# Seven of 36 probability tiles per group turned through memory instead of on TensorE

## The chip, the cores and the metric

One core of one Trainium2 chip runs the whole program. The metric is the device time of one launch in microseconds. The core has five engines that this text names by their short forms: PE (TensorE, matrix products), DVE (VectorE), ACT (ScalarE), POOL (GpSimd) and SP (SyncE, which issues DMAs). ACT can issue DMAs too, on a queue of its own.

## The reference

The input x is (2, 1024, 512) in float32: two batches of 1024 tokens. The result is x plus an attention block, and then that plus a small mixture of low-rank products:

```python
x = x + attn(layernorm(x), Wq, Wk, Wv, Wo, q_norm_w, k_norm_w)
x = x + ffn(layernorm(x), A, B, Wr, br)
# attn: 32 query heads, 8 key/value heads, head size 128
q, k = rmsnorm(x @ Wq.T) , rmsnorm(x @ Wk.T); v = x @ Wv.T
scores = q . k / sqrt(128) + slope * (pos_k - pos_q), causal
out = softmax(scores) @ v ;  return out @ Wo.T
# ffn: 8 experts of rank 16, gated by a softmax of x @ Wr.T
```

Everything is computed in float32 accuracy. The kernel gets this from a faster matrix format by splitting each operand into an upper and a lower part (`_hi`, `_lo`) and adding three products.

## The kernel before

The work is cut into 16 groups: 8 key/value heads for the first batch (w = 0 to 7) and the same 8 for the second (w = 8 to 15). A group has 4 query heads. Its 1024 query tokens are 8 tiles of 128, numbered s = 0 to 7. Because attention is causal, tile s has s + 1 blocks of 128 key tokens, so a group has 1 + 2 + ... + 8 = 36 probability tiles, each holding 128 queries by 128 keys for 4 heads (128 x 512 numbers).

For each s the steps are: `scores` (PE, one per head), `max` (DVE), `exp` (ACT), `invert` (DVE, reciprocal of the sum), `normalise` (POOL, one per head). A product with v needs the probabilities with keys in the partitions, so each tile (s, j) is turned: `turn.p.s.j` is four 128 x 128 transposes on PE into a PSUM bank, `high.p.s.j` on ACT writes the upper part `pT_hi`, `low.p.s.j` on DVE writes the rest `pT_lo`, and `values.s.j` is the three products on PE that add to `o_ps`. Then come `o_high`, `o_low` and `y.s` (12 products with Wo), and `add_y`. The next group's projections (`q`, `turn.kv`) and the turns of its weights (`turn.wkv`, `turn.wq`, `turn.wo`) are mixed in between. The turned weights of the first batch are written to memory (`keep_*`) and read back in the second (`back_*`), so the second batch turns none.

The order of the work is written out by hand as lists of names, one list for each kind of group: `PROLOGUE`, `GROUP_A` (w = 0 to 6), `BOUNDARY` (w = 7), `FIRST_B` (w = 8), `GROUP_B` (w = 9 to 14), `LAST` (w = 15). Each engine walks through the list in order and takes the names that are its own (`follow`); it can't go past an item whose semaphore is not there yet. Three PSUM banks (`turn_ps`) take all turns in a ring. The tiles of `pT` are a ring of three too:

```python
r = piece(s, j) % RING
after(pe, "low", "p", w, s, j)
split_product(o_ps[:], [((v_hi[:, j, :], v_lo[:, j, :]), (pT_hi[:, r, :], pT_lo[:, r, :]))],
              start=j == 0, stop=j == s).then_inc(sems["values"], 1)
```

All large DMAs are issued by SP, from one queue. `wq_raw`, `wo_raw` and `wkv_raw` are separate buffers for raw weights.

Of the kernel before, what the change touches and what calls it, by code (L numbers as in the profile page):

```python
# [21 lines left out]

PROLOGUE = (
# [1083 lines left out]
```

## Time and profile before

| | us |
|---|---|
| median of 3 runs | 2157.64 (2156.7 to 2157.95) |
| profiled execution, whole | 2155.97 |
| its span | 2154.1 |
| PE busy in the span | 2122.3 (99%) |
| DVE busy | 1359.1 (63%) |
| ACT busy | 1145.4 (53%) |
| POOL busy | 787.0 (37%) |

The profile is of one execution. Busy time is the time in which an engine had an instruction under way. Its span leaves out 1.87 us of the execution's own time. TensorE's granted clock was 0.998 of full speed. The chain of waits follows the work that ended last back to its start.

### The profile page before, as it was taken

How to read it: one execution, taken by the hardware profiler on the slowest of the kernel's cores; microseconds unless marked ns; L12 is line 12 of the kernel's file. 1: busy time of each engine (PE TensorE's matmuls, PEld its weight loads, DVE VectorE, ACT ScalarE, POOL GpSimd, SP SyncE). 2: the span in 40 equal slices, each digit the busy share in tenths (PEclk: the TensorE clock that was granted, in tenths of full speed). 3: DMA queues.
4: the chain of work that ended last, by engine and by line, in shares of the span. 5: the costliest groups of instructions: out<-in, count | busy, mean ns of one | idle time of the engine just before them, and what ended most of it. 6: DMA issues, size and time to landing. Idle time of an engine off the chain costs nothing.

```text
span 2154.1 us, 33327 instructions
## 1 busy us (share of the span) xinstructions
PE 2122.3 (99%) x12220; PEld 1825.0 (85%) x12220; DVE 1359.1 (63%) x3431; ACT 1145.4 (53%) x3314; POOL 787.0 (37%) x872
## 2 busy tenths in 40 slices
PE   7999999999999999999999999999999999999997
PEld 6888888888888888888888888888888888888885
DVE  6566665666565666668765656565565656566676
ACT  4555555565555655555545555554555555555552
POOL 3343333334333442334333334242432424244341
PEclk9999999999999999999999999999999999999999
DMA  5121200212102120112120111111011111101101
GB/s 176 50 98 50 99 27 23 99 50 98 50 23 76 50 98 40 60 46 82 55 103 28 51 40 40 60 40 59 1 59 40 40 59 40 42 18 40 40 1 39
DMA packets 32128, 118.01 MB, mean 55 GB/s; under 512 B 4184, under 2 KB 4184, under 8 KB 23776
## 3 DMA queue, kind: packets, MB, share of 16 engines
q1 hardware_dynamic: 31536, 115.89, 14.5%
q8 instruction: 98, 1.61, 0.3%
q14 instruction: 62, 0.51, 0.1%
...
## 4 chain that ended last, share of the span: by engine, by line
PE 97%; DVE 1%; ACT 1%; issue 0%; DMA 0%; POOL 0%; SPq 0%; POOLq 0%; DVEq 0%; ACTq 0%
PE s_ps L926 19%; PE o_ps L926 18%; PE turn_ps L1013 17%; PE y_ps L926 17%; PE q_ps L926 16%; PE turn_ps L926 9%; PE y_ps L1082 1%; PE turn_ps L1007 1%; DMA wkv_raw<-in_L_attn_Wv 0%; DVE oT_lo L851 0%; ACT oT_hi L662 0%; DVE pT_lo L810 0%; SPq L555 0%; ACT pT_hi L634 0%; DVE y L857 0%
## 5 line engine op out<-in xcount | busy, mean ns | idle before, releaser
L719 POOL TENSOR_TENSOR probs<-probs,p_inv 128x896 f32<-128x896 f32 (+7 forms) x512 | 578.5, 1151 | 690.3 <-DVE p_inv L830 690.2
L634 ACT ACTIVATE pT_hi<-turn_ps 128x512 fp32r<-128x512 f32 x576 | 339.5, 598 | 357.2 <-PE turn_ps L1013 357.0
L810 DVE TENSOR_TENSOR pT_lo<-turn_ps,pT_hi 128x512 fp32r<-128x512 f32 x576 | 391.0, 686 | 206.7 <-ACT pT_hi L634 204.5
L823 DVE CUSTOM_DVE_ANT_0 probs<-s_ps,rel 128x896 f32<-128x896 f32 (+7 forms) x512 | 383.0, 752 | 188.3 <-issue 187.1
L641 ACT ACTIVATE probs<-probs,neg_max 128x640 f32<-128x640 f32 (+7 forms) x512 | 397.3, 778 | 157.0 <-DVE neg_max L823 155.9
L1013 PE MATMUL turn_ps<-ident,probs 128*128 128x128 f32 x2336 | 342.9, 273 | 7.7 <-DVE probs L750 7.6
L1013 PEld LDWEIGHTS turn_ps<-ident,probs 128*128 128x128 f32 x2336 | 286.9, 141 | 71.7 <-issue 10.7
L926 PE MATMUL s_ps<-kT_hi,qT_hi 128*128 128x512 f32 (+3 forms) x768 | 273.5, 356 | 1.0 <-DVE qT_lo L812 0.4
L926 PE MATMUL s_ps<-kT_hi,qT_lo 128*128 128x512 f32 (+3 forms) x768 | 262.7, 342 | 0.0
L926 PE MATMUL s_ps<-kT_lo,qT_hi 128*128 128x512 f32 (+3 forms) x768 | 262.0, 341 | 0.0
L926 PE MATMUL o_ps<-pT_hi,v_hi 128*128 128x512 f32 x576 | 246.9, 429 | 1.2 <-DVE oT_lo L851 1.0
L926 PE MATMUL o_ps<-pT_hi,v_lo 128*128 128x512 f32 x576 | 226.8, 394 | 0.0
L926 PE MATMUL o_ps<-pT_lo,v_hi 128*128 128x512 f32 x576 | 226.4, 393 | 0.0
L926 PE MATMUL q_ps<-wqT_hi,xnT_hi 128*128 128x512 f32 x512 | 220.8, 431 | 1.0 <-DVE qn L834 1.0
L926 PE MATMUL y_ps<-woT_hi,oT_hi 128*128 128x512 f32 x512 | 208.3, 407 | 2.3 <-DVE oT_lo L851 1.9
L692 POOL TENSOR_TENSOR q_sum_eps<-q_sum,q_eps 128x4 f32<-128x4 f32 x128 | 26.5, 207 | 480.5 <-ACT qn L650 480.5
L926 PE MATMUL q_ps<-wqT_hi,xnT_lo 128*128 128x512 f32 x512 | 201.6, 394 | 0.0
L926 PE MATMUL q_ps<-wqT_lo,xnT_hi 128*128 128x512 f32 x512 | 201.0, 393 | 0.0
L926 PE MATMUL y_ps<-woT_hi,oT_lo 128*128 128x512 f32 x512 | 200.5, 392 | 0.0
L926 PE MATMUL y_ps<-woT_lo,oT_hi 128*128 128x512 f32 x512 | 199.9, 391 | 0.0
L662 ACT ACTIVATE oT_hi<-o_ps 128x512 fp32r<-128x512 f32 x128 | 76.4, 597 | 167.2 <-PE o_ps L926 164.9
L926 PEld LDWEIGHTS s_ps<-kT_hi,qT_hi 128*128 128x128 f32 x768 | 144.7, 188 | 21.9 <-DVE neg_max L823 0.8
...
## 6 DMA issues: line engine op xcount, KB each, us to landing
wq_raw<-in_L_attn_Wq SPq DMA_DIRECT2D x8, 1024.0 KB, 11.7
wq_kept<-wqT_hi SPq DMA_DIRECT2D x8, 1024.0 KB, 3.9
wq_kept<-wqT_lo SPq DMA_DIRECT2D x8, 1024.0 KB, 7.7
wo_raw<-in_L_attn_Wo SPq DMA_DIRECT2D x8, 1024.0 KB, 10.0
wo_kept<-woT_hi SPq DMA_DIRECT2D x8, 1024.0 KB, 5.3
wo_kept<-woT_lo SPq DMA_DIRECT2D x8, 1024.0 KB, 7.3
wqT_hi<-wq_kept SPq DMA_DIRECT2D x8, 1024.0 KB, 4.8
wqT_lo<-wq_kept SPq DMA_DIRECT2D x8, 1024.0 KB, 6.9
```

The source lines that it names most:

```text
L634: nc.scalar.activation(target, bank, ACT.Copy).then_inc(sems["high"], 1)
L641: nc.scalar.activation(row, row, ACT.Exp, bias=neg_max[:, s % 2, h:h + 1], scale=-1.0, accum_out=p_sum[:, s % 2, h:h + 1]).then_inc(sems[" ...
L662: nc.scalar.activation(oT_hi[:].rearrange("p h n -> p (h n)"), o_ps[:], ACT.Copy).then_inc(sems["o_high"], 1)
L692: nc.gpsimd.tensor_tensor(sum_eps, source, eps, ALU.add).then_inc(sum_eps_done, 1)
L719: nc.gpsimd.tensor_tensor(row, row, p_inv[:, s % 2, h:h + 1].to_broadcast((P, L)), ALU.mult).then_inc(sems["normalise"], 1)
L810: nc.vector.tensor_tensor(target, bank, upper.bitcast(F32), ALU.subtract).then_inc(sems["low"], 1)
L823: nc.vector.tensor_tensor_reduce(out=probs[:, s % 2, h, 0:L], in0=s_ps[:, at_col:at_col + L], in1=rel[:, S - L:S], scale=-float(slopes[w % ...
L926: last = nc.tensor.matmul(target, a, m, start=start and i == 0 and k == 0, stop=stop and i == len(pairs) - 1 and k == 2)
L1007: last = nc.tensor.matmul(bank[:, 0:P + NE], f_x[:, t % 2, c * P:(c + 1) * P], arT[:, c, :], start=c == 0, stop=c == C - 1)
L1013: last = nc.tensor.transpose(bank[0:width, i * rows:(i + 1) * rows], source, ident[0:rows, 0:rows])
L1082: nc.tensor.matmul(y_ps[:], low_turned[:, t % 2, :], bT[:], start=True, stop=True).then_inc(sems["f_out"], 1)
```

## The change

Tile (5,5), tiles (6,5) and (6,6), and tiles (7,4) to (7,7) of each group are no longer turned on PE. Their probabilities go from SBUF to a scratch tensor in memory (`send_p`, one DMA for each head), come back as 32 x 32 blocks in exchanged places (`fetch_p`, four DMAs for each tile, one for each 32 target partitions, in runs of 32 numbers = 128 bytes), DVE turns the numbers inside each block (`flip_p`), ACT makes the upper part (`upper_p`) and POOL the lower part (`lower_p`). A tile's `values` comes after those of the tiles that PE turns. Seven tiles in 16 groups are 112 tiles, or 448 transposes of 128 x 128.

```diff
+MEMORY_TILES = {5: (5,), 6: (5, 6), 7: (4, 5, 6, 7)}
+    TURN_SLOTS, MEMORY_SLOTS, RAW_TILES = 2, 2, 3
+    def values_order(s):
+        return [j for j in range(s + 1) if j not in through_memory(s)] + through_memory(s)
-        wq_raw = sb("wq_raw", [P, G, DM])
-        wkv_raw = sb("wkv_raw", [P, 2, DM])
-        wo_raw = sb("wo_raw", [P, C, W512])
+        w_raw = sb("w_raw", [P, G + 2, DM])
+        p_raw = sb("p_raw", [P, RAW_TILES, G * P])
-        pT_hi = sb("pT_hi", [P, RING, G * P], F32R)
+        pT_hi = sb("pT_hi", [P, TURN_SLOTS + MEMORY_SLOTS, G * P], F32R)
+        p_bounce = nc.dram_tensor("p_bounce", [2, NT, G, P, P], F32).ap()
...
+            def send_p(w, s, h):
+                first = through_memory(s)[0]
+                before = [name for name in sent if name[1] % 2 == s % 2 and sent[name] == sent[w, s] - 16 * G]
+                if before and h == 0:
+                    after(sp, "flip_p", *before[0], through_memory(before[0][1])[-1])
+                after(sp, "normalise", w, s, h)
+                sp.dma_start(p_bounce[s % 2, first:s + 1, h].rearrange("u p c -> p u c"),
+                             probs[s % 2][:, h, first * P:(s + 1) * P].rearrange("p (u c) -> p u c", c=P)).then_inc(p_sent[s % 2], 16)
+            def fetch_p(w, s, j):
+                n = fetch_number[w, s, j]
+                sp.wait_ge(p_sent[s % 2], sent[w, s])
+                if n >= RAW_TILES:
+                    after(sp, "lower_p", *p_fetch[n - RAW_TILES])
+                blocks = p_bounce[s % 2, j].rearrange("h (a i) (b j) -> b i (h a) j", i=BLOCK, j=BLOCK)
+                for b in range(NBLK):
+                    sp.dma_start(p_raw[b * BLOCK:(b + 1) * BLOCK, n % RAW_TILES, :].rearrange("p (n j) -> p n j", j=BLOCK),
+                                 blocks[b]).then_inc(p_fetched[n % RAW_TILES], 16)
...
+            def flip_p(w, s, j):
+                n = fetch_number[w, s, j]
+                dve.wait_ge(p_fetched[n % RAW_TILES], 16 * NBLK * (n // RAW_TILES + 1))
+                raw = p_raw[:, n % RAW_TILES, :]
+                nc.vector.transpose(raw, raw).then_inc(sems["flip_p"], 1)
...
+            def upper_p(w, s, j):
+                after(act, "flip_p", w, s, j)
+                if p_before[w, s, j]:
+                    after(act, "values", *p_before[w, s, j])
+                nc.scalar.activation(pT_hi[:, p_slot[w, s, j], :], p_raw[:, fetch_number[w, s, j] % RAW_TILES, :],
+                                     ACT.Copy).then_inc(sems["upper_p"], 1)
...
+            def lower_p(w, s, j):
+                r = p_slot[w, s, j]
+                after(pool, "upper_p", w, s, j)
+                nc.gpsimd.tensor_tensor(pT_lo[:, r, :], p_raw[:, fetch_number[w, s, j] % RAW_TILES, :], pT_hi[:, r, :].bitcast(F32),
+                                        ALU.subtract).then_inc(sems["lower_p"], 1)
```

The room for `p_raw` comes from the raw weights: Wq and Wo of a group now share one buffer, so Wq of group w + 1 is loaded after `turn.wo` of w, and Wo of w + 1 after `turn.wq` of w + 1. After the first ones, all `load_w*`, `keep_*` and `back_*` are issued by ACT, at their places in the lists, with the same waits before them:

```diff
+            def load_wq(w, *first):
+                if not first and w + 1 < NG:
+                    after(act, "turn", "wo", w, G - 1)
+                    act.dma_start(w_raw[:, 0:G, :], wq_v[w + 1]).then_inc(wq_loaded, 16)
+            def load_wo(w, *first):
+                if not first and w + 1 < NG:
+                    after(act, "turn", "wq", w + 1, C - 1)
+                    act.dma_start(w_raw[:, 0:G, :], wo_v[w + 1]).then_inc(wo_loaded, 16)
+            def keep_wq(w):
+                after(act, "low", "wq", w + 1, C - 1)
+                act.dma_start(wq_kept[w + 1, 0], wqT_hi[:].rearrange("p c n -> p (c n)").bitcast(F32)).then_inc(wq_spilled, 16)
+                act.dma_start(wq_kept[w + 1, 1], wqT_lo[:].rearrange("p c n -> p (c n)").bitcast(F32)).then_inc(wq_spilled, 16)
```

All six lists are new. This is the end of `GROUP_A`:

```
send_p.7.3 low.p.6.4 lower_p.6.6 values.6.3 inv_q.8 fetch_p.7.4 values.6.4 turn.p.7.0 values.6.5 high.p.7.0
fetch_p.7.5 turn.p.7.1 low.p.7.0 values.6.6 high.p.7.1 turn.kv.2 load_wo low.p.7.1 o_high.6 fetch_p.7.6
norm_q.8 o_low.6 values.7.0 high.kv.2 values.7.1 keep_wq low.kv.2 turn.p.7.2 flip_p.7.4 q.9.0 upper_p.7.4
turn.p.7.3 high.p.7.2 turn.kv.3 lower_p.7.4 high.p.7.3 low.p.7.2 flip_p.7.5 fetch_p.7.7 low.p.7.3 upper_p.7.5
flip_p.7.6 lower_p.7.5 turn.q.8 high.kv.3 values.7.2 high.q.8 low.kv.3 inv_k values.7.3 keep_wkv low.q.8
values.7.4 add_y.5 values.7.5 upper_p.7.6 flip_p.7.7 q.9.1 lower_p.7.6 norm_k upper_p.7.7 y.6 lower_p.7.7
values.7.6 add_y.6 turn.k.0 values.7.7 high.k.0 turn.k.1 o_high.7 q.9.2 high.k.1 o_low.7 q.9.3 v_high low.k.0
y.7 low.k.1 square_q.9 v_low inv_q.9 add_y.7
```

The same stretch of `GROUP_B`, which loads and keeps no weights there:

```
send_p.7.3 square_q.8 low.p.6.4 flip_p.6.6 upper_p.6.6 values.6.3 lower_p.6.6 fetch_p.7.4 add_y.5 values.6.4
turn.p.7.0 inv_q.8 values.6.5 high.p.7.0 fetch_p.7.5 turn.p.7.1 low.p.7.0 values.6.6 high.p.7.1 turn.kv.3
low.p.7.1 o_high.6 fetch_p.7.6 o_low.6 flip_p.7.4 upper_p.7.4 flip_p.7.5 lower_p.7.4 values.7.0 high.kv.3
values.7.1 low.kv.3 inv_k turn.p.7.2 fetch_p.7.7 turn.p.7.3 high.p.7.2 y.6 high.p.7.3 low.p.7.2 upper_p.7.5
low.p.7.3 lower_p.7.5 flip_p.7.6 norm_q.8 values.7.2 norm_k values.7.3 values.7.4 flip_p.7.7 values.7.5
upper_p.7.6 turn.q.8 lower_p.7.6 upper_p.7.7 q.9.0 high.q.8 turn.k.0 low.q.8 lower_p.7.7 turn.k.1 high.k.0
q.9.1 add_y.6 high.k.1 values.7.6 low.k.0 values.7.7
```

In `PROLOGUE`, SP's loads came in the order y.0, y.1, y.3, Wq, y.2, y.6, y.4, Wkv; they now come as y.4, y.0, y.1, y.5, Wkv, y.3, Wq.

## Rows read from the trace of the kernel before

**Rows 1.** The page: busy time and share of the span by engine, chain by engine.

```profile
PE 2122.3 (99%) x12220; PEld 1825.0 (85%) x12220; DVE 1359.1 (63%) x3431; ACT 1145.4 (53%) x3314; POOL 787.0 (37%) x872
...
PE 97%; DVE 1%; ACT 1%; issue 0%; DMA 0%; POOL 0%; SPq 0%; POOLq 0%; DVEq 0%; ACTq 0%
```

**Rows 2.** Busy time by engine in one period of GROUP_A, one of GROUP_B.

```profile
core 0: us, PE busy (x) PEld busy (x) DVE busy (x) ACT busy (x) POOL busy (x), PEclk, DMA share, GB/s
301.94:433.38 131.44, 131.38 (x765) 113.63 (x765) 81.39 (x198) 72.56 (x210) 47.42 (x50) 1.00 0.16 61
1371.31:1497.88 126.57, 126.57 (x726) 109.28 (x726) 76.86 (x189) 68.44 (x200) 47.42 (x50) 1.00 0.11 42
```

**Rows 3.** PE in order of time: start, duration, instruction; one turn among products.

```profile
535.26 0.40 PE L926 MATMUL o_ps<-pT_lo,v_hi 128*128 128x512 f32 x1
535.50 0.39 PE L926 MATMUL o_ps<-pT_hi,v_lo 128*128 128x512 f32 x1
535.73 0.60 PE L1013 MATMUL turn_ps<-ident,probs 128*128 128x128 f32 x4
536.08 0.48 PE L926 MATMUL q_ps<-wqT_hi,xnT_hi 128*128 128x512 f32 x1
536.39 0.40 PE L926 MATMUL q_ps<-wqT_lo,xnT_hi 128*128 128x512 f32 x1
```

**Rows 4.** The chain in order of time: one turn.kv, start and length.

```profile
547.93 2.87 PE turn_ps L926 x24
```

**Rows 5.** Groups by line and shape: busy us, mean ns, idle before, releaser.

```profile
L810 DVE TENSOR_TENSOR pT_lo<-turn_ps,pT_hi 128x512 fp32r<-128x512 f32 x576 | 391.0, 686 | 206.7 <-ACT pT_hi L634 204.5
L1013 PE MATMUL turn_ps<-ident,probs 128*128 128x128 f32 x2336 | 342.9, 273 | 7.7 <-DVE probs L750 7.6
L634 ACT ACTIVATE pT_hi<-turn_ps 128x512 fp32r<-128x512 f32 x576 | 339.5, 598 | 357.2 <-PE turn_ps L1013 357.0
L719 POOL TENSOR_TENSOR probs<-probs,p_inv 128x512 f32<-128x512 f32 x64 | 65.5, 1048 | 45.1 <-DVE p_inv L830 45.1
```

**Rows 6.** POOL in order of time: normalise.7.0 to 7.3 of one group.

```profile
535.50 3.75 POOL L719 TENSOR_TENSOR probs<-probs,p_inv 128x1024 f32<-128x1024 f32 x2 [6.10 <-DVE p_inv L830]
541.57 3.75 POOL L719 TENSOR_TENSOR probs<-probs,p_inv 128x1024 f32<-128x1024 f32 x2 [1.08 <-DVE p_inv L830]
```

**Rows 7.** The page's DMA issues: count, KB each, median us to landing.

```profile
woT_hi<-wo_kept SPq DMA_DIRECT2D x8, 1024.0 KB, 4.8
woT_lo<-wo_kept SPq DMA_DIRECT2D x8, 1024.0 KB, 7.2
out<-y SPq DMA_DIRECT2D x16, 256.0 KB, 2.3
wkv_raw<-in_L_attn_Wk SPq DMA_DIRECT2D x8, 256.0 KB, 2.7
wkv_raw<-in_L_ffn_B SPq DMA_DIRECT2D x1, 256.0 KB, 5.4
```

**Rows 8.** SP's queue in order of time: how long issuing a DMA takes.

```profile
511.56 0.44 SPq L523 DMA_DIRECT2D wq_kept<-wqT_lo  x1
513.00 2.10 SPq L517 DMA_DIRECT2D wkv_kept<-wkvT_hi  x1
```

**Rows 9.** DMA packets from 972.5 to 973.0 us, while B is loaded.

```profile
DMA packets 425, 0.15 MB, mean 298 GB/s; under 512 B 402, under 2 KB 402, under 8 KB 425
q1 hardware_dynamic: 425, 0.15, 118.5%
```

**Rows 10.** The start: SP's issues, and PE's first work.

```profile
5.37 0.47 SPq L499 DMA_DIRECT2D wkv_raw<-in_L_attn_Wv  x1
...
7.63 2.28 PE L1013 MATMUL turn_ps<-ident,probs 128*128 128x128 f32 x8 [7.63 <-DVE probs L750]
13.01 1.12 PE L1013 MATMUL turn_ps<-ident,wkv_raw 128*128 128x128 f32 x4 [3.10 <-DMA wkv_raw<-in_L_attn_Wv]
```

More of the change, by code:

```diff
@@ L300, in attention_lora_block, with through_memory @@
         plans.setdefault(w, group_a if w < NG else group_b)
+    def through_memory(s):
+        return list(MEMORY_TILES.get(s, ()))
+    def values_order(s):
+        return [j for j in range(s + 1) if j not in through_memory(s)] + through_memory(s)
     def ffn_batch(w):
@@ L338, in attention_lora_block @@
             number[named(w, *item)] = counted[item[0]]
+    p_slot, p_before, p_fetch, sent = {}, {}, [], {}
+    turned, flipped, sends = [], [], [0, 0]
+    for w in range(-1, LAST_W + 1):
+        for item in plans[w]:
+            if item[:2] == ("turn", "p"):
+                p_slot[(w, *item[2:])] = len(turned) % TURN_SLOTS
+                turned.append((w, *item[2:]))
+            elif item[0] == "flip_p":
+                p_slot[(w, *item[1:])] = TURN_SLOTS + len(flipped) % MEMORY_SLOTS
+                p_before[(w, *item[1:])] = flipped[-MEMORY_SLOTS] if len(flipped) >= MEMORY_SLOTS else None
+                flipped.append((w, *item[1:]))
+            elif item[0] == "send_p" and item[2] == G - 1:
+                sends[item[1] % 2] += 16 * G
+                sent[w, item[1]] = sends[item[1] % 2]
+            elif item[0] == "fetch_p":
+                p_fetch.append((w, *item[1:]))
+    fetch_number = {name: n for n, name in enumerate(p_fetch)}
     def follow(work):
@@ L455, in attention_lora_block @@
         sems = {kind: sem(f"{kind}_done") for kind in counted}
+        p_sent = [sem("p_sent_even"), sem("p_sent_odd")]
+        p_fetched = [sem(f"p_fetched{i}") for i in range(RAW_TILES)]
         ident_ready = sem("ident_ready")
@@ L501, in load_wq @@
-            def load_wq(w, *first):
-                g = 0 if first else w + 2
-                if g < NG:
-                    if not first:
-                        after(sp, "turn", "wq", g - 1, C - 1)
-                    sp.dma_start(wq_raw[:], wq_v[g]).then_inc(wq_loaded, 16)
-            def load_wo(w, *first):
-                g = 0 if first else w + 1
-                if g < NG:
-                    if not first:
-                        after(sp, "turn", "wo", g - 1, G - 1)
-                    sp.dma_start(wo_raw[:], wo_v[g]).then_inc(wo_loaded, 16)
@@ new lines, in load_wq @@
+            def load_wq(w, *first):
+                if first:
+                    sp.dma_start(w_raw[:, 0:G, :], wq_v[0]).then_inc(wq_loaded, 16)
+            def load_wo(w, *first):
+                if first:
+                    after(sp, "turn", "wq", 0, C - 1)
+                    sp.dma_start(w_raw[:, 0:G, :], wo_v[0]).then_inc(wo_loaded, 16)
+            def send_p(w, s, h):
[6 more added lines that the diff above has]
+                             probs[s % 2][:, h, first * P:(s + 1) * P].rearrange("p (u c) -> p u c", c=P)).then_inc(p_sent[s % 2], 16)
@@ L579, in store @@
                 sp.dma_start(out_v[b, :, t, :], y[:, t, :]).then_inc(stored[t], 16)
-            follow({"load_wkv": load_wkv, "load_wq": load_wq, "load_wo": load_wo, "keep_wkv": keep_wkv, "keep_wq": keep_wq,
-                    "keep_wo": keep_wo, "back_wkv": back_wkv, "back_wq": back_wq, "back_wo": back_wo, "load_y": load_y,
+            follow({"load_wkv": load_wkv, "load_wq": load_wq, "load_wo": load_wo, "send_p": send_p, "fetch_p": fetch_p, "load_y": load_y,
                     "load_x": load_x, "load_a": load_a, "load_wr": load_wr, "load_b": load_b, "store": store})
@@ L591, in _, with load_wkv @@
             act.dma_start(br_row[:], br.rearrange("(a n) -> a n", a=1).broadcast_to((P, NE))).then_inc(small_loaded, 16)
+            def load_wkv(w, *first):
+                if not first and w + 2 < NG:
+                    after(act, "turn", "wkv", w + 1, 1)
+                    act.dma_start(w_raw[:, G, :], wk_v[w + 2]).then_inc(wkv_loaded, 16)
+                    act.dma_start(w_raw[:, G + 1, :], wv_v[w + 2]).then_inc(wkv_loaded, 16)
+            def load_wq(w, *first):
+                if not first and w + 1 < NG:
+                    after(act, "turn", "wo", w, G - 1)
+                    act.dma_start(w_raw[:, 0:G, :], wq_v[w + 1]).then_inc(wq_loaded, 16)
@@ new lines, in load_wo, with keep_wkv @@
+            def load_wo(w, *first):
+                if not first and w + 1 < NG:
+                    after(act, "turn", "wq", w + 1, C - 1)
+                    act.dma_start(w_raw[:, 0:G, :], wo_v[w + 1]).then_inc(wo_loaded, 16)
+            def keep_wkv(w):
+                after(act, "low", "wkv", w + 1, 1)
+                act.dma_start(wkv_kept[w + 1, 0], wkvT_hi[:].rearrange("p c n -> p (c n)").bitcast(F32)).then_inc(wkv_spilled, 16)
+                act.dma_start(wkv_kept[w + 1, 1], wkvT_lo[:].rearrange("p c n -> p (c n)").bitcast(F32)).then_inc(wkv_spilled, 16)
@@ L598, in high @@
                 if of == "p":
[L599 removed]
+                    target = pT_hi[:, p_slot[w, *which], :]
                 elif of == "q":
@@ L672, in sort_b @@
                 nc.scalar.activation(b_sorted.rearrange("p o h r -> p h o r"), b_raw, ACT.Copy).then_inc(sems["sort_b"], 1)
-            follow({"high": high, "exp": exp, "square_q": square_q, "v_high": v_high,
+            follow({"load_wkv": load_wkv, "load_wq": load_wq, "load_wo": load_wo, "keep_wkv": keep_wkv, "keep_wq": keep_wq,
+                    "keep_wo": keep_wo, "back_wkv": back_wkv, "back_wq": back_wq, "back_wo": back_wo, "high": high, "upper_p": upper_p, "exp": exp, "square_q": square_q, "v_high": v_high,
                     "o_high": o_high, "f_exp": f_exp, "sort_b": sort_b})
@@ L717, in normalise @@
                     after(pool, "invert", w, s, h // 2)
-                row = probs[:, s % 2, h, 0:L]
+                row = probs[s % 2][:, h, 0:L]
                 nc.gpsimd.tensor_tensor(row, row, p_inv[:, s % 2, h:h + 1].to_broadcast((P, L)),
                                         ALU.mult).then_inc(sems["normalise"], 1)
-            follow({"inv_q": inv_q, "inv_k": inv_k, "x_rstd": x_rstd, "f_rstd": f_rstd, "normalise": normalise})
+            def lower_p(w, s, j):
[3 more added lines that the diff above has]
+                                        ALU.subtract).then_inc(sems["lower_p"], 1)
+            follow({"lower_p": lower_p, "inv_q": inv_q, "inv_k": inv_k, "x_rstd": x_rstd, "f_rstd": f_rstd, "normalise": normalise})
         @block.vector
@@ L760, in low @@
                     plain = f_logits[:, which[0] % 2, :]
+                    if which[0] >= 2:
+                        after(dve, "f_low", ffn_batch(w), which[0] - 2)
                 elif of == "lora":
@@ L786, in low @@
                 if of == "p":
-                    r = piece(*which) % RING
+                    r = p_slot[w, *which]
                     target, upper = pT_lo[:, r, :], pT_hi[:, r, :]
@@ L873, in f_norm @@
                     after(dve, "turn", "logits", 0, NT - 2 + t)
+                else:
+                    after(dve, *(("turn", "b") if t else ("sort_b", NG - 1)))
                 after(dve, "f_rstd", b, t)
@@ L941, in turn @@
                     s, j = which
-                    if j == 0:
+                    if j == values_order(s)[0]:
                         after(pe, "normalise", w, s, G - 1)
-                    sources = [probs[:, s % 2, h, j * P:(j + 1) * P] for h in range(G)]
+                    sources = [probs[s % 2][:, h, j * P:(j + 1) * P] for h in range(G)]
                 elif of == "q":
@@ L956, in turn @@
                         pe.wait_ge(wkv_loaded, 32 * (w + 2))
-                    sources = [wkv_raw[:, m, c * P:(c + 1) * P] for c in (2 * which[0], 2 * which[0] + 1) for m in range(2)]
+                    sources = [w_raw[:, G + m, c * P:(c + 1) * P] for c in (2 * which[0], 2 * which[0] + 1) for m in range(2)]
                 elif of == "wq":
@@ L960, in turn @@
                         pe.wait_ge(wq_loaded, 16 * (w + 2))
-                    sources = [wq_raw[:, h, which[0] * P:(which[0] + 1) * P] for h in range(G)]
+                    sources = [w_raw[:, h, which[0] * P:(which[0] + 1) * P] for h in range(G)]
                 elif of == "wo":
@@ L964, in turn @@
                         pe.wait_ge(wo_loaded, 16 * (w + 1))
-                    sources = [wo_raw[:, c, which[0] * P:(which[0] + 1) * P] for c in range(C)]
+                    sources = [w_raw[:, c, which[0] * P:(which[0] + 1) * P] for c in range(C)]
                 elif of == "x":
@@ L1053, in values @@
             def values(w, s, j):
-                if j == 0:
+                order = values_order(s)
+                if j == order[0]:
                     if s == 0:
@@ L1058, in values @@
                         after(pe, "o_low", w - (s == 0), (s - 1) % NT)
-                r = piece(s, j) % RING
-                after(pe, "low", "p", w, s, j)
+                r = p_slot[w, s, j]
+                if j in through_memory(s):
+                    after(pe, "lower_p", w, s, j)
+                else:
+                    after(pe, "low", "p", w, s, j)
                 split_product(o_ps[:], [((v_hi[:, j, :], v_lo[:, j, :]), (pT_hi[:, r, :], pT_lo[:, r, :]))],
-                              start=j == 0, stop=j == s).then_inc(sems["values"], 1)
+                              start=j == order[0], stop=j == order[-1]).then_inc(sems["values"], 1)
             def y_product(w, s):
```

118 lines of the change are left out of this document (55 added, 63 removed), and 481 rows, old and new, of tables (BOUNDARY, FIRST_B, GROUP_A, GROUP_B).

## The prediction, on record before the changed kernel ran

> **What bounds the kernel now.** I read the page's busy shares and its chain first [rows 1]. PE is busy for 2122.3 of 2154.1 us, and the chain of waits runs through PE for 97% of the span. No other engine is above 63%. Then I looked at one period of each common kind of group [rows 2]: the first batch's takes 131.44 us with PE busy for 131.38, the second batch's takes 126.57 with PE busy for all of it. DVE is busy for 81 and 77 us, ACT for 73 and 68, POOL for 47. So almost every microsecond is PE's own work. Anything removed from PE's stream shortens the period, as long as nothing new makes PE wait. The question is what a tile that leaves PE must pass through and whether it is back in time.
>
> **What a turn is worth on PE.** The groups by line put 342.9 us on 2336 transposes [rows 5], 0.147 each, 0.59 for a tile. But PE's instructions overlap, so I read starts [rows 3]. A product starts at 535.50, the turn at 535.73, the next product at 536.08, the one after that at 536.39. Products follow each other every 0.23 to 0.24 us. The turn thus takes 0.35 and delays the second product by another 0.08: 0.43 us. A third reading agrees roughly: a GROUP_A period holds ten turns of weights more than a GROUP_B period (40 more instructions, 765 against 726 with one record missing) and lasts 4.87 us longer [rows 2], 0.49 a turn. I take 0.43, the directly read start times, and keep 0.59 for the range. 112 turns x 0.43 = 48.7 us less, 3.05 us a group. By 0.59 it would be 65.8.
>
> **What the other engines get.** Counted per memory tile: DVE's `low` (0.686) becomes `flip_p` on the same 128 x 512 numbers. No DVE transpose is in the trace. I take 0.69, with half and double as ends: 7 x 0.69 = 4.8 us in a group at double, beside 45 us in which DVE is idle. ACT's `high` (0.598) becomes `upper_p` from SBUF, taken the same. POOL gets `lower_p`, new work, nearest to `normalise` of 512 columns, 1.05 us [rows 5]: 7 x 1.05 = 7.3 us a group, POOL 55 of 128 us. ACT gets the issues of the weight DMAs, ten in a first-batch group, six in a second-batch one. An issue takes 0.44 us, and 2.10 with much queued in front [rows 8]: 4 us a group, up to 10. ACT has 58 us idle. None of this costs time by its amount. It costs by where an in-order engine stands still, so the chain of a memory tile decides.
>
> **The chain of a tile, and the room for it.** Is a place in the list a time? I summed PE's work up to an item: a product of three matmuls 0.69 (3 x 0.23, from rows 3), `y` 2.75 (12 x 0.23), `turn.kv` 2.87 [rows 4], a turn 0.43. For the old list that puts normalise.7.0 at 535.7 and normalise.7.3 at 544.0; the trace has 535.50 and 543.4 [rows 6]. So lists give times within a microsecond or two.
>
> The tightest case is s = 7. Only three raw tiles exist, so fetch_p.7.7 waits for lower_p.7.4. Two round trips in a row must fit between send_p.7.3 and values.7.7. PE's work between these is, in GROUP_A, 11 x 0.69 (values) + 2 x 0.69 (q) + 6 x 0.43 + 2 x 2.87 + 2.75 = 20.2 us. In GROUP_B it is 17.7 (one `turn.kv` and one turn more instead of the second `turn.kv`). The same count gives 19.7 in BOUNDARY and in FIRST_B, 15.2 in LAST.
>
> The need is the send's landing, then twice (fetch + flip + upper + lower). The send: 2.3 us, as for a store of 256 KB [rows 7]. Flip, upper and lower: 0.69 + 0.60 + 1.05 + 0.1 = 2.45. The fetch X: four issues, the last one starting 1.3 us after the first, and the nearest load of 256 KB lands in 2.7 [rows 7], together 4.0. It moves 2048 packets of 128 bytes where that load moved 128 of 2 KB. What a small packet costs shows once: while B was loaded, 425 packets, 402 of them under 512 bytes, passed in 0.5 us over 16 engines [rows 9]. At that rate 2048 packets need 2.4 us, most of it beside the issues. I take X = 4.4. Bounds: 2.7 below (as a plain load), 10.8 above (B's 1024 small packets landed 5.4 us after issue, behind other traffic [rows 7]; twice that). I stay near the low end, because the 5.4 contains the queue ahead of B and the 0.5 us of rows 9 doesn't.
>
> Need = 2.3 + 2 x (4.4 + 2.45) = 16.0 us. It fits GROUP_A by 4.2, the two middle lists by 3.7, GROUP_B by 1.7, and misses LAST by 0.8. DVE stands at each `flip_p` until its tile has landed, and behind it wait `low` of turned tiles, and PE for those through only two slots and three banks. I allow for such small stalls: 1.0 us in each of 7 GROUP_A (more DMAs on ACT and the shared weight buffer), 0.3 in 6 GROUP_B, 0.5 each in BOUNDARY and FIRST_B, 0.8 in LAST: 10.6. The earlier tiles have more room: tile (5,5) has its fetch 17.7 us before its values in GROUP_A, 15.9 in GROUP_B.
>
> **A rule of the skill against this.** The B row shows many small runs moving at near 300 GB/s [rows 9]. The Trainium skill (VectorE: DVE Perf Modes, "The three transpose paths") warns that a plain DMA whose access pattern does the transpose is 19 times slower than the crossbar one where the innermost destination stride is large. Here each run is 128 contiguous bytes on both sides and DVE does the inner part, so I read the rule as not met; no run here shows the crossbar path. Were it met, by that page's shares (my estimate) a tile would take some 11 us and the kernel would be slower, as in the first rival.
>
> **The weights' queue.** Wq's shared buffer leaves its load from about 16 us into a group until turn.wq.0 near 55, and Wo's from 108 until the next group's start, 19 us. A megabyte more takes 2.4 us (7.2 - 4.8, rows 7), so both arrive in time: cost 0. If the cover went, a late Wo would hold PE for what is missing.
>
> **The start.** PE's first weight turn starts at 13.01, held by the Wkv load, whose second DMA SP issued at 5.37 behind 1 MB of Wq and seven or so loads of x [rows 10]. Now 1.5 MB, not 3, go up to it, 3.7 us less at 2.4 us a megabyte, but Wq is then what comes last. I take 3 us less, bounds 0 and 4.
>
> **Sum.** Against the profiled execution: 2155.97 - 48.7 - 3.0 + 10.6 = 2114.9. The median of the runs is 1.67 above that execution: 2116.6, I say 2116.
>
> **Rivals.**
> *Small packets are dear* (slower). If X is long, s = 7 stalls PE in every group. With need 7.2 + 2X, the stalls over 16 groups are 16 x (7.2 + 2X) less the sum of the rooms, 7 x 20.2 + 6 x 17.7 + 2 x 19.7 + 15.2 = 302.2. They eat the 51.7 us won where 7.2 + 2X = 22.1, X = 7.5. At X = 8 the stalls are 69 us: 2155.97 - 51.7 + 69 + 1.7 = 2175. At 10.8: 2265. For it: no row has 128-byte packets, and DVE standing at flips may add. Against: the rate of rows 9.
> *The bulk on ACT's queue collides* (smaller gain). In GROUP_A load_wo, keep_wq and keep_wkv, 4 MB, are issued at the time of fetches 7.6 and 7.7. If the DMA engines alternate between the queues packet by packet, 128 small packets on each wait behind big ones until the bulk is gone. From fetch_p.7.7 to values.7.7 PE has 7.8 us of work; 4.4 + 2.45 are needed, and up to 5.4 of bulk remain: 4.5 late. With up to 2 us for ACT held in an issue [rows 8] that is 6.5 x 7 = 45.5 in place of 7: 2155. With half of it, 2132. For it: row and list put them together. Against: the bulk is issued in parts and lands at 2.4 us a megabyte. The Trainium skill (DMA: Bandwidth & Descriptors, "Issuing engines are not separate DMA queues") says that DMAs from several engines share the same 16 engines and interleave, which speaks for the collision; no row of before shows two large queues at once.
> *No stall, and the turn is worth more.* 2157.64 - 48.7 - 3 = 2106 without stalls; with 0.59 a turn, 2089.
>
> **Chances.** Forecast (2102 to 2128): 0.58. Full gain, under 2102: 0.12. Collision, 2128 to 2153: 0.14. At or near no change, the two rivals' edge: 0.04. Dear packets, slower: 0.12. I give 2098 to 2150 as the range. 0.2% is 4.3 us, about what can be told from no change here: faster 0.84, same 0.03, slower 0.13.
>
> **What would show it.** Right: 448 fewer transposes of `probs`; periods near 128.5 to 129.5 us in the first batch and 123.7 to 124.5 in the second; `p_raw` landing about 3 us after each issue; DVE's wait at `p_raw` short; PE idle under 1 us a group. Dear packets: fetches of 6 us or more, PE idle in front of `o_ps` for `pT_lo` from POOL in every group. Collision: that only in first-batch groups, with fetches 7.6 and 7.7 longer than 7.4. My forecast is wrong if PE's idle time in a GROUP_B period is over 2 us, or if a removed turn shortens the period by less than 0.35.

## The result, and the profile after

The changed kernel takes 2137.64 us (median of 4 runs, 2135.65 to 2138.16), the kernel before 2157.30 beside it (4 runs). The ratio is 0.991, with a 95% interval of 0.9897 to 0.9922. That is 19.7 us faster where 41 were forecast. The profiled execution of after has a span of 2136.3 us, 17.8 under that of before.

The page of after: busy time by engine, and the chain by engine, as in [rows 1].

```profile
PE 2083.0 (98%) x11772; PEld 1786.4 (84%) x11772; DVE 1355.6 (63%) x3431; ACT 1148.2 (54%) x3314; POOL 936.1 (44%) x984
...
PE 83%; DVE 4%; issue 4%; DMA 3%; SPq 2%; POOL 2%; ACT 2%; ACTq 0%; DVEq 0%; POOLq 0%
```

448 PE instructions are gone, as the change says. PE's share of the chain fell from 97% to 83%, and DMA and SP's queue stand in it now. Which part of the kernel they hold up is seen by group. I took each period from the first score product of one group to that of the next, in both traces (us):

```
stage                 before   after   difference   forecast
start, to group 0      42.70   40.26      -2.44       -3.0
7 first-batch groups  919.58  922.29      +2.71      -14.4
BOUNDARY              150.01  146.91      -3.10       -2.6
FIRST_B               135.18  131.10      -4.08       -2.6
6 second-batch groups 759.39  748.68     -10.71      -16.5
LAST, to the end      147.24  147.06      -0.18       -2.3
```

Five of the six stages became shorter. The seven first-batch groups, which lose as many turns as the others, became longer. Two of their periods, then a second-batch one (columns as in [rows 2], whose two periods they answer to):

```profile
174.15:306.70 132.55, 129.60 (x739) 111.88 (x738) 81.23 (x199) 73.11 (x209) 56.87 (x58) 0.99 0.30 88
306.70:437.38 130.68, 128.22 (x740) 110.73 (x738) 81.24 (x199) 73.12 (x209) 56.91 (x58) 1.00 0.30 89
1365.46:1490.24 124.78, 123.89 (x698) 106.81 (x696) 75.64 (x188) 68.13 (x199) 56.64 (x57) 1.00 0.26 73
```

PE is idle for 2.95 and 2.46 us in the first two, 0.89 in the third; before it was 0.06 and 0. In the first of them PE's busy time is 1.4 us higher at the same work, and the mean clock 0.99. The waits of after, PE's (engine, line, releaser: us in total, times, longest):

```profile
PE y_ps L1026 <- DVE y L955: 16.6, 7, 2.9
PE turn_ps L1113 <- DVE probs_odd L836: 8.6, 1, 8.6
PE q_ps L1026 <- DVE qn L932: 6.9, 8, 0.9
```

The second is in the start and stood in before too (7.6). The first comes once in each first-batch group, the third at the start of each second-batch one. How the first comes about is in the chain of the first group's tail (start, length, what; the two SPq rows are the issues of the second and third part of fetch_p.7.6):

```profile
148.78 0.87 SPq L568
149.65 0.04 issue
149.69 1.82 SPq L568
151.51 0.04 issue
151.55 8.73 DMA p_raw<-p_bounce
160.28 0.02 issue
160.31 0.04 DVE p_raw L907
160.34 0.60 issue
160.94 0.65 DVE kv_raw L871
161.59 0.65 DVE qT_lo L900
162.25 0.61 DVE y L955
162.85 0.14 issue
162.99 4.58 PE y_ps L1026 x12
```

Issuing the third part of fetch_p.7.6 took SP 1.82 us instead of 0.49, so the fourth went out at 151.55 only, and landed 8.73 us after that. The whole fetch took 12.0 us from its first issue (148.30), where the fetch before the tail's bulk, 7.4, took 3.8. DVE stood at flip_p.7.6 for it. Behind that flip stood low.kv.3, low.q.8 and add_y.5, which empties the bank that y.6 needs. The DMA issues of the same 24 us, 144 to 168 (KB each, median us to landing):

```profile
q10 hardware_dynamic: 1104, 4.19, 46.0%
q1 hardware_dynamic: 8448, 1.05, 28.2%
...
p_raw<-p_bounce SPq DMA_DIRECT2D x16, 64.0 KB, 5.0
w_raw<-in_L_attn_Wo ACTq DMA_DIRECT2D x1, 1024.0 KB, 6.1
wq_kept<-wqT_hi ACTq DMA_DIRECT2D x1, 1024.0 KB, 6.6
wq_kept<-wqT_lo ACTq DMA_DIRECT2D x1, 1024.0 KB, 8.8
```

q1 is SP's queue (packets, MB, share of 16 engines), q10 ScalarE's. The same 16 parts in a second-batch tail, 1462 to 1486, with no bulk beside them:

```profile
p_raw<-p_bounce SPq DMA_DIRECT2D x16, 64.0 KB, 2.2
```

And the stretches around the wait (PE busy and count, ..., PEclk, DMA share, GB/s). While fetch 7.6 is under way the share of the 16 DMA engines is 1.20 and 1.04, so they have no free time; behind the wait PE's clock is at half:

```profile
158.00:160.00 2.00, 2.00 (x10) 1.66 (x9) 0.00 (x0) 0.00 (x0) 1.20 (x1) 1.00 1.20 303
160.00:162.00 2.00, 0.41 (x2) 0.00 (x0) 1.69 (x3) 0.63 (x1) 0.24 (x1) 1.00 1.04 386
162.00:163.00 1.00, 0.01 (x1) 0.04 (x1) 0.84 (x2) 0.00 (x0) 1.00 (x1) 1.00 0.58 105
163.00:164.00 1.00, 1.00 (x3) 0.86 (x4) 0.00 (x1) 0.00 (x0) 0.03 (x1) 0.68 0.05 8
164.00:165.00 1.00, 1.00 (x4) 0.71 (x3) 1.00 (x2) 0.25 (x1) 0.00 (x0) 0.50 0.00 0
165.00:166.00 1.00, 1.00 (x4) 0.81 (x3) 0.82 (x1) 0.38 (x1) 0.55 (x1) 0.50 0.00 0
166.00:167.00 1.00, 1.00 (x5) 0.77 (x4) 0.00 (x0) 0.00 (x0) 0.95 (x1) 0.62 0.00 0
167.00:168.00 1.00, 1.00 (x6) 0.83 (x5) 0.32 (x1) 0.00 (x0) 0.00 (x0) 1.00 0.00 0
```

PE ran at 1.2 instead of 2.4 GHz from 163.4 to 166.8, after an idle time of 2.58 us (the next group's, 2.95, had the same effect). So y.6 took 4.42 us from its first start to what follows it, against 2.90 for y.7 in a second-batch group. This happened in 4 of the 7 groups.

### The profile page after: what moved, and what is told of

It is laid out like the page before. It is cut to its first block, busy times and chain, and to the rows that moved or that the text cites. A ratio compares the mean times of both kernels' runs of the same rounds, so it can differ in the third digit from the quotient of the medians.

```text
span 2136.3 us, 33509 instructions
## 1 busy us (share of the span) xinstructions
PE 2083.0 (98%) x11772; PEld 1786.4 (84%) x11772; DVE 1355.6 (63%) x3431; ACT 1148.2 (54%) x3314; POOL 936.1 (44%) x984
## 4 chain that ended last, share of the span: by engine, by line
PE 83%; DVE 4%; issue 4%; DMA 3%; SPq 2%; POOL 2%; ACT 2%; ACTq 0%; DVEq 0%; POOLq 0%
PE s_ps L1026 17%; PE q_ps L1026 15%; PE y_ps L1026 15%; PE o_ps L1026 15%; PE turn_ps L1113 13%; PE turn_ps L1026 5%; DMA p_raw<-p_bounce 3%; SPq L568 2%; POOL probs_odd L799 1%; PE turn_ps L1107 1%; PE y_ps L1186 1%; DVE pT_lo L898 1%; DMA p_bounce<-probs_odd 1%; DVE y L955 0%; DVE oT_lo L949 0%
## 5 line engine op out<-in xcount | busy, mean ns | idle before, releaser
L799 POOL TENSOR_TENSOR probs_odd<-probs_odd,p_inv 128x256 f32<-128x256 f32 (+3 forms) x256 | 316.4, 1256 | 326.9 <-DVE p_inv L928 326.9
L706 ACT ACTIVATE pT_hi<-turn_ps 128x512 fp32r<-128x512 f32 x464 | 271.6, 597 | 316.2 <-PE turn_ps L1113 315.9
L799 POOL TENSOR_TENSOR probs_even<-probs_even,p_inv 128x128 f32<-128x128 f32 (+3 forms) x256 | 261.8, 1044 | 386.1 <-DVE p_inv L928 386.1
L898 DVE TENSOR_TENSOR pT_lo<-turn_ps,pT_hi 128x512 fp32r<-128x512 f32 x464 | 314.6, 684 | 146.2 <-ACT pT_hi L706 145.2
L921 DVE CUSTOM_DVE_ANT_0 probs_odd<-s_ps,rel 128x256 f32<-128x256 f32 (+3 forms) x256 | 209.3, 820 | 131.9 <-issue 131.4
L1026 PE MATMUL s_ps<-kT_hi,qT_hi 128*128 128x512 f32 (+3 forms) x768 | 278.7, 363 | 2.6 <-DVE kT_lo L900 1.8
L720 ACT ACTIVATE probs_odd<-probs_odd,neg_max 128x256 f32<-128x256 f32 (+3 forms) x256 | 211.9, 832 | 76.0 <-DVE neg_max L921 75.9
L921 DVE CUSTOM_DVE_ANT_0 probs_even<-s_ps,rel 128x128 f32<-128x128 f32 (+3 forms) x256 | 174.0, 686 | 118.0 <-issue 117.2
L720 ACT ACTIVATE probs_even<-probs_even,neg_max 128x128 f32<-128x128 f32 (+3 forms) x256 | 184.4, 721 | 76.6 <-DVE neg_max L921 75.7
L805 POOL TENSOR_TENSOR pT_lo<-p_raw,pT_hi 128x512 fp32r<-128x512 f32 x112 | 145.5, 1306 | 182.2 <-ACT pT_hi L714 181.5
L1026 PE MATMUL y_ps<-woT_hi,oT_hi 128*128 128x512 f32 x512 | 206.8, 404 | 18.7 <-DVE y L955 16.6
```

Source lines behind the costliest of these rows:

```text
L706: nc.scalar.activation(target, bank, ACT.Copy).then_inc(sems["high"], 1)
L720: nc.scalar.activation(row, row, ACT.Exp, bias=neg_max[:, s % 2, h:h + 1], scale=-1.0, accum_out=p_sum[:, s % 2, h:h + 1]).then_inc(sems[" ...
L799: nc.gpsimd.tensor_tensor(row, row, p_inv[:, s % 2, h:h + 1].to_broadcast((P, L)), ALU.mult).then_inc(sems["normalise"], 1)
L805: nc.gpsimd.tensor_tensor(pT_lo[:, r, :], p_raw[:, fetch_number[w, s, j] % RAW_TILES, :], pT_hi[:, r, :].bitcast(F32), ALU.subtract).then_ ...
L898: nc.vector.tensor_tensor(target, bank, upper.bitcast(F32), ALU.subtract).then_inc(sems["low"], 1)
L921: nc.vector.tensor_tensor_reduce(out=probs[s % 2][:, h, 0:L], in0=s_ps[:, at_col:at_col + L], in1=rel[:, S - L:S], scale=-float(slopes[w % ...
```

## The experiments

Beside every experiment the kernel before ran on the same chip, with a median of 2156.0 to 2156.4 us. My theory: the collision. ScalarE's bulk transfers delay the read-backs of 7.6 and 7.7, DVE stands, PE waits and then runs at half clock. The rivals: the small packets or SP's issues are slow by themselves; DVE's order is at fault; a turn is worth less than forecast.

### The bulk moved out of the tail

```
 # in GROUP_A
- ... flip_p.6.6 load_wkv ... turn.kv.2 load_wo ... values.7.1 keep_wq ... values.7.3 keep_wkv ...
+ ... max.2.1 load_wkv keep_wkv load_wq ... high.p.5.0 load_wo keep_wq q.8.0 ...
```

> The changed kernel, with the bulk transfers of a first-batch group moved away from its tail: load_wkv and keep_wkv stand before load_wq (about 16 us into the group), load_wo and keep_wq after high.p.5.0 (about 70 us in). The same bytes, the same engine and queue; only the last 25 us of a group are free of them. Theory (bulk transfers delay the read-backs of 7.6 and 7.7): a read-back lands in some 2.3 us instead of a median of 5.0, VectorE no longer stands 4.5 us at flip_p.7.6, the products wait under 0.5 us for y.6 instead of 1.8 to 2.9, and the granted clock stays at 1.00 behind it. First-batch periods 129.0 (128.5 to 129.5) instead of 130.6 to 133.9, some 2.9 us each over 7: whole kernel 2117 (2112 to 2122). Rival (the 128-byte packets themselves, or SyncE's issues, are the limit): nothing changes at the tail, periods 130.6 to 133.9, whole kernel 2135 to 2140. Rival (the stretch the bulk is moved to pays): tail clean, but a wait at 16 or 70 us as long, whole kernel 2130 to 2140.

Measured (e1): 2112.71 us (2111.84 to 2113.62), ratio 0.9798 (0.9784 to 0.9813). The tail of the first group, 144 to 168, and the second and fourth periods:

```profile
q1 hardware_dynamic: 8448, 1.05, 27.7%
...
p_raw<-p_bounce SPq DMA_DIRECT2D x15, 64.0 KB, 2.3
```

```profile
169.18:296.92 127.74, 127.74 (x739) 110.85 (x738) 81.40 (x199) 73.06 (x209) 57.57 (x58) 1.00 0.32 91
425.71:553.46 127.75, 127.75 (x740) 110.86 (x738) 81.26 (x199) 73.12 (x209) 57.58 (x58) 1.00 0.32 91
```

The same 1.05 MB of small packets land in 2.3 us, PE has no idle time, and the clock stays at 1.00. The seven periods sum to 895.7, 26.6 under those of after. Bytes, packets and queues are the same, so the small packets alone are not the cause, and the coincidence is. That the bulk stretch pays instead fell too, but not because nothing collides there. load_wo and keep_wq now stand beside fetch_p.5.5; the transfers of 100 to 125 show its four parts:

```profile
p_raw<-p_bounce SPq DMA_DIRECT2D x4, 64.0 KB, 6.8
```

The whole of fetch 5.5 takes 12.6 to 14.3 us in the seven groups, longer than 7.6 did in the tail of after (11.2 to 12.4). PE doesn't wait for it: tile (5,5) is the one that the prediction gave 17.7 us of room. So the bulk went from a fetch without room to one with room. The period is even shorter than I expected, 127.75 for 129.0.

### Which of the bulk

```
e8:  load_wkv keep_wkv before load_wq; load_wo, keep_wq stay
e9:  load_wo keep_wq after high.p.5.0; load_wkv, keep_wkv stay
e14: keep_wq alone after high.p.5.0; the other three stay
```

> The changed kernel with only load_wkv and keep_wkv moved to the start of a first-batch group; load_wo and keep_wq stay in its tail beside the read-backs of 7.4 to 7.7. Of the tail's 4.2 MB of bulk 3 MB stay, 1 MB and ScalarE's last two issues go. If the time the bulk takes from the small packets is what counts, about a quarter of the 25 us goes: 2131 (2126 to 2135). If only the transfer beside 7.7's read-back matters (keep_wkv is issued at 157.0, flip_p.7.6 waits from 155.8), most of it goes: 2115 to 2122.

> The changed kernel with only load_wo and keep_wq (3 MB) moved out of a first-batch group's tail; load_wkv and keep_wkv (1.5 MB, keep_wkv beside the read-back of 7.7) stay there. By the run that moved the others alone and gained under 2 us, nearly all of the 25 us hangs on these two: 2113 to 2118. If the two pairs each suffice to spoil the tail, 2128 to 2136.

> The changed kernel with only keep_wq (2 MB, two issues) moved; load_wo (1 MB, issued 4 us earlier) and the first projection's transfers stay. If what counts is the bytes on the DMA engines while 7.6 is read back, two thirds of them go and with them most of the wait, and the half clock behind it: 2116 to 2124. If load_wo alone is enough, since it slows the read-backs of 7.5 and 7.6 and SyncE's issues behind them: 2128 to 2136.

Measured: e8 2135.69 us (2132.39 to 2137.35), e9 2113.83 (2113.30 to 2113.92), e14 2110.48 (2108.95 to 2110.68). The seven first-batch periods sum to 921.5, 896.7 and 896.3 (after 922.3, e1 895.7): keep_wq alone, 2.1 MB of 4.2, makes all of it, more than I had expected of it. The 3.4 us by which e14 beats e9 are not the tail's: in the profiled executions 3.05 of them lie in LAST, whose list is the same in both. With keep_wq gone, load_wo and keep_wkv stay in the tail at no price, though load_wo still makes fetch 7.5 take 7.5 us instead of 3.9. The transfers of e14 there, and DVE's work in order of time:

```profile
p_raw<-p_bounce SPq DMA_DIRECT2D x16, 64.0 KB, 2.4
w_raw<-in_L_attn_Wo ACTq DMA_DIRECT2D x1, 1024.0 KB, 6.0
wkv_kept<-wkvT_hi ACTq DMA_DIRECT2D x1, 512.0 KB, 3.0
```

```profile
155.92 0.69 DVE L908 STREAM_TRANSPOSE p_raw<-p_raw 128x512 f32<-128x512 f32 x1
157.45 0.69 DVE L872 COPY kv_raw<-turn_ps 128x512 f32<-128x512 f32 x1 [0.84 <-ACT kv_raw L697]
158.06 0.74 DVE L901 SCALAR_TENSOR_TENSOR qT_lo<-turn_ps,wq_norm,qT_hi 128x512 fp32r<-128x512 f32 x1
158.72 0.68 DVE L956 TENSOR_TENSOR y<-y_ps,y 128x512 f32<-128x512 f32 x1
```

The flip starts at 155.92 instead of 160.31, add_y.5 at 158.72 instead of 162.17: in time for y.6. In after, keep_wq is issued at 150.75 and 151.12, while SP still issues the third part of fetch_p.7.6 and before the fourth (151.55).

### One queue instead of two

```
 # load_wkv, load_wq, load_wo, keep_*, back_*, at the same places of the order
- act.dma_start(...)
+ sp.dma_start(...)
```

> The changed kernel, with the later weight loads, write-backs and read-backs issued by SyncE at the same places of the order instead of by ScalarE: ScalarE issues no DMA. Bulk and small transfers then stand on one queue. If it is the issuing engine (ScalarE's issues of 0.4 to 2 us in front of its exp and high items, and back_wkv late at a group's start) that costs, the second-batch groups lose the 0.83 us wait for norm_q.1 and the first-batch groups gain about 1 us: 2122 to 2130. If it is the DMA engines' shared time, 2134 to 2140. If one queue puts the small read-backs behind whole bulk transfers (1 MB each), first-batch periods grow by 3 to 10 us: 2155 to 2200. I hold the last the likeliest.

Measured (e2): 2122.10 us (2121.42 to 2122.39), ratio 0.9841. The likeliest of my three was wrong: the same bulk in the same tail on one queue costs less, 15.5 us less over the kernel. The first group's tail, SP's issues and the transfers:

```profile
148.86 2.94 SPq L568 DMA_DIRECT2D p_raw<-p_bounce  x4
151.85 1.99 SPq L624 DMA_DIRECT2D wq_kept<-wqT_hi  x1
153.88 2.28 SPq L625 DMA_DIRECT2D wq_kept<-wqT_lo  x1
156.25 3.56 SPq L568 DMA_DIRECT2D p_raw<-p_bounce  x4
```

```profile
p_raw<-p_bounce SPq DMA_DIRECT2D x16, 64.0 KB, 2.9
```

Fetch 7.6 now stands ahead of keep_wq in one queue, and its flip started at 156.80. It takes 7.9 us where it took 12.0 on two queues. Fetch 7.7 is behind keep_wq and late (its flip at 162.63). PE's waits for y.6 are gone, but PE is still idle for 6.7 us over the seven groups, 3.5 in front of turn.k.0 and 3.0 for pT_lo from POOL: both stand behind fetch 7.7. The seven periods sum to 907.3, 15.0 under after and 11.6 over e1, so one queue gives back a little more than half. The second-batch periods did not move (124.8), so the 0.83 us at their start is not ScalarE's issues. The Trainium skill (DMA: Bandwidth & Descriptors, "Issuing engines are not separate DMA queues") says that DMAs started by several engines interleave on the same 16, and that a second issuer saves only sequencer time. The trace agrees: beside ScalarE's bulk SP's parts land in a median of 5.0 us instead of 2.2. The same bulk behind and before them in one queue makes it 2.9.

### DVE's order alone

```
 # in GROUP_A
- ... flip_p.7.5 ... flip_p.7.6 ... add_y.5 ...
+ ... add_y.5 flip_p.7.5 ... flip_p.7.6 ...
```

> The changed kernel, with add_y.5 of a first-batch group moved before flip_p.7.5 in VectorE's order, so that it no longer stands behind flip_p.7.6 and its transfer; nothing else changes. Theory (the late transfer reaches the products only through VectorE's order): the wait for y.6 (1.8 to 2.9 us in each of the 7) goes, part of it comes back at values.7.6, which needs the same read-back, but the stretch at granted clock 0.50 (1.6 to 1.8 us in 4 of 7) goes if the rest is short: periods 130.0 to 130.8, whole kernel 2129 (2124 to 2134). Rival (the read-back itself is what the products end on): the wait moves to values.7.6 at the same length, 2135 to 2140.

Measured (e3): 2139.38 us (2137.12 to 2142.36), the same as after. PE's waits:

```profile
PE turn_ps L1113 <- issue: 12.3, 7, 1.9
...
PE o_ps L1026 <- POOL pT_lo L805: 3.7, 10, 0.5
```

The waits for y went, and a wait of 1.5 to 1.9 us in each of the 7 groups took their place, at the transposes of kv_raw (turn.k.0, whose norm_k stands behind flip_p.7.7). The granted clock still fell to half behind 4 of the 7. The late read-backs are the cause; the order only chooses who waits. I had the new place wrong (values.7.6).

### The second-batch groups' start

```
 # end of FIRST_B and GROUP_B; norm_q.1 leaves the start of GROUP_B and LAST
- ... inv_q.9 add_y.7
+ ... inv_q.9 norm_q.9 add_y.7
```

> The changed kernel, with norm_q.1 taken from the start of each second-batch group and put, as norm_q.9 of the group before, ahead of add_y.7 in VectorE's order. Theory (the 0.83 us by which a second-batch group's idle time rose is add_y.7 in front of norm_q.1): the wait q_ps <- DVE qn of 0.9 us goes in the 7 starts, second-batch periods 124.0 instead of 124.8, whole kernel 2132 (2130 to 2134). Rival (square_q.9 and inv_q.9 are themselves late, as turn.kv.0 no longer fills the gap): the wait stays at 0.6 or more, 2136 to 2138.

Measured (e4): 2134.51 us (2130.22 to 2138.61), with the collision still in: in the profiled execution the second group waits 6.2 us for y.6 alone. The second-batch periods tell more than the total. Five of the six are 123.94 to 123.96 each in place of 124.74 to 124.78; the first of them (w = 9) stays at 124.9.

```profile
PE q_ps L1027 <- DVE qn L933: 1.9, 2, 1.0
```

The wait had been DVE's add_y.7 (1490.51, 0.69 us) in front of norm_q.1 (1491.11), where PE's score products were over at 1491.02. Before, a turn.kv stood between. The theory stands for six of the seven starts. At w = 9 the wait stays at 0.95 us: there DVE is free, and norm_q.9 starts at 1246.98 because it waits for inv_q.9 on POOL, as the rival said.

### The price of a turn by itself

```
- for i, source in enumerate(sources):
+ again = of == "p" and tuple(which) in TWICE   # 7 tiles a group
+ for i, source in list(enumerate(sources)) * (2 if again else 1):
```

> Both reorderings (2105.7 us), with seven of the tiles that TensorE still turns (5.1, 5.3, 6.0, 6.2, 6.4, 7.1, 7.3) turned twice into the same bank: 112 turns of four 128x128 transposes more, no item, wait or transfer more. It measures the price of a turn by itself. By the forecast's 0.43 us a turn: +48 us, 2154, second-batch periods 126.9. By the second-batch groups' own difference (2.63 us over 7, 0.376): +42 us, 2148, 126.6. By the first-batch groups' (3.65 over 7, 0.52): +58 us, 2164. If some of it falls into gaps in which TensorE waits anyway, less than 35 us.

Measured (e13): 2151.15 us (2150.02 to 2153.76, 9 runs). That is 45.4 us over both reorderings alone (e5, below), 0.405 a turn. By stage: 0.437 in the seven first-batch groups (916.53 - 895.13 over 49), 0.419 in five second-batch ones (126.86 - 123.93 over 7), 1.5 us for seven in LAST. The forecast's 0.43 holds in the groups that make up most of the kernel.

### Both reorderings, and variants of them

```
e5:  load_wkv keep_wkv before load_wq; load_wo keep_wq after high.p.5.0; norm_q.9 before add_y.7
e10: e5, and in load_*, keep_*, back_*:  - act.dma_start(...)   + sp.dma_start(...)
e15: keep_wq after high.p.5.0; norm_q.9 before add_y.7
e7:  e5, LAST's list from the kernel before, and
- return list(MEMORY_TILES.get(s, ()))
+ return list(MEMORY_TILES.get(s, ())) if w < LAST_W else []
```

> The changed kernel with both reorderings at once: the first-batch bulk transfers moved out of the group's tail, and norm_q.1 put ahead of add_y.7. If the two losses are separate waits their gains add up: first-batch periods 127.8 as with the bulk moved alone, second-batch periods 123.9 as with norm_q.1 moved alone, LAST 0.9 shorter: 2112.7 - 6 = 2107 (2105 to 2109). If one only hid the other: 2110 to 2113.

> Both reorderings, and the later bulk transfers issued by SyncE instead of ScalarE. If the queue mattered only through the collision, nothing is left for it to gain: the same as both reorderings alone, 2107 (2105 to 2110). If ScalarE's issues delay its items elsewhere, 1 to 3 us faster. If SyncE's longer list delays the read-backs (its waits for high and low items stand in front of fetch items), 3 to 10 us slower.

> The changed kernel with keep_wq alone moved out of the first-batch tail, and norm_q.1 put ahead of add_y.7. If the two gains add as they did before (6 to 7 us for norm_q.1): 2110.5 - 6.7 = 2104 (2102 to 2106), the fastest of all. If load_wo and the first projection's transfers in the tail still cost something that two reorderings hide: 2106 to 2109.

> Both reorderings, and in the last group alone the order of the kernel before: all its 36 tiles turned on TensorE, no round trips there. If the trips in the last group bring what they bring elsewhere (2.6 to 3.6 us), this is 2 to 4 us slower than both reorderings alone, 2110. If the end of the kernel hangs on the feed-forward chain on VectorE, so that TensorE time freed there turns into waiting, as the 0.18 us of the changed kernel says, it is within 1 us: 2106 to 2108. With the norm_q.1 gain of 0.9 in both, I hold the second the likelier.

Measured: e5 2105.74 us (2105.43 to 2107.14), ratio to before 0.9769 (0.9755 to 0.9782); e10 (issued by SP) 2105.48 (2105.42 to 2105.99); e15 (only keep_wq and norm_q.1 moved) 2107.06 (2104.79 to 2109.09); e7 (LAST all on PE) 2106.90 (2106.03 to 2107.64). The two gains add in e5. In e15 they fell short of my 2104: 2107.06 is in the rival's range, and not to be told from e5 within its spread. A period of e5 in each batch:

```profile
296.29:424.04 127.75, 127.75 (x739) 110.78 (x738) 81.34 (x199) 73.08 (x209) 57.58 (x58) 1.00 0.32 91
1462.11:1586.05 123.94, 123.88 (x698) 106.80 (x697) 75.64 (x188) 68.13 (x199) 56.64 (x58) 1.00 0.26 73
```

With the collision gone the queue makes no difference. e7's last stage lasts 146.4 us against e5's 146.1, which is no difference: one and the same list of LAST took 145.4 us (e14) to 148.5 (e9) in single executions, with the granted clock at half for 6.0 and 13.3 us of it. The fair pair is e15 and e7, at half clock for 9.4 and 9.2 us. With the trips PE is busy for 131.3 us and idle for 14.7, without them 133.5 and 12.9. Seven turns less save 2.1 us of PE's work in LAST, and 1.8 come back as waiting. e5 beats both kernels, by 31.9 us the changed one and by 50.3 the one before.

## Why the prediction was wrong

**The price of a turn** (0.43): right, 0.405 to 0.437 when measured alone. Removing seven brought 3.68 us in an undisturbed first-batch period (131.43 to 127.75) and 2.63 in a second-batch one (126.57 to 123.94), 0.53 and 0.38 each. The mean is near 0.43; the orders differ as well, and what in them makes 0.53 of the one and 0.38 of the other is open. Two slips in the sums moved the forecast by 0.5 us at most: 112 x 0.43 is 48.2, not 48.7, and the room in GROUP_A adds up to 20.0, not 20.2.

**The chain of a tile**: right where nothing else moves. A flip took 701 ns (I had taken 0.69), an upper 631 (0.60). The lower took 1306, not 1048: the nearest row was a product with a broadcast factor, and this one reads two whole tiles. It was off the path. A part of a fetch lands in 2.2 to 2.3 us. A whole one with its issues takes 3.5 to 4.2 us with nothing beside it (I took 4.4) and up to 5.1 in the second-batch groups, and the tight s = 7 holds there without a stall. The rival of dear packets is refuted: periods 123.94 and 127.75 hold all of them. The rule of the Trainium skill weighed there (VectorE: DVE Perf Modes, "The three transpose paths") was not met by runs of 128 bytes: a tile alone takes 3.5 to 4.2 us with its four issues, far from the 11 that I had worked out for it. No run here shows the crossbar path, so the factor itself is not measured.

**The stalls allowed**: here it failed. The step is "1.0 us in each of 7 GROUP_A", which rests on X = 4.4 us for every fetch. Beside the bulk, fetch 7.6 took 11.2 to 12.4 us in the seven groups and 7.7 took 8.8 to 9.5. Measured are 922.29 - 895.13 = 27.2 us over e5, 3.9 a group in place of 1.0. Of them 16.6 are the waits for y, some 6 are y.6 at half clock (4 x 1.5). Another 1.6 have nothing to do with the collision: at the start of the first group the clock is at half from 40.5 to 43.9, which e5 lacks and e14 has (first period 129.46, against 127.88 in e1, which lacks it too). Some 3 I can't place row by row. This is the rival "the bulk on ACT's queue collides", and the total landed inside its 2128 to 2153, which had 0.14. The mechanism I described there is the one found, with three differences. The transfer that matters is keep_wq, not the sum of 4 MB. It strikes at fetch 7.6 and reaches PE through add_y.5 and y.6, not through values.7.7. And the half clock behind the wait was in neither the rival nor the bounds. What I held against it (parts that land at 2.4 us a megabyte) was no reason: 2.4 us a megabyte is what the bulk needs, and two such megabytes are 4.8 us beside a fetch that has room for 4.2 in all. The sum of rooms counted the fetch as if it were alone, although the list puts both in the same stretch.

**GROUP_B, 0.3 a group**: PE's idle time is 0.89 us in five periods and 1.01 in the first, 5.5 where 1.8 stood. It is the wait for norm_q.1, which follows from the new order and not from the tiles' transfers; moving norm_q.1 takes 0.84 (124.78 - 123.94) off each of the five. The other 2.1 us missing there are the turns, at 0.38 instead of 0.43. My own test (PE idle over 2 us in a period) did not trip.

**The start**: 2.44 for 3.0. **The weights' queue at 0**: right for the loads, and wrong for keep_wq, which I had priced only as an issue on ACT. **BOUNDARY and FIRST_B**: 0.5 and 1.5 better than forecast. **LAST**: -0.18 instead of -2.3, from one execution each of a stage that varies by 3 us. PE's busy time fell by 1.6 us only, since the clock was at half for 13.7 us of it instead of 9.2, and its idle time rose by 1.5. The second part is the step that failed, and e7 against e15 shows it at equal clock: of 2.1 us saved 1.8 come back as idle time. PE waits there for the feed-forward chain through DVE (6.3 us of its idle time in LAST of after are waits for low_gated and low_turned). I had charged it 3.05 less 0.8 like any other group.

By stage the 23.5 us missing in the profiled execution are 17.1 first-batch groups, 5.8 second-batch ones, 2.1 LAST and 0.6 the start, less 2.1 in BOUNDARY and FIRST_B.
